# The reciprocal of the softmax sums of an attention kernel, taken in a dense 128x16 layout between DMAs

## What is computed

```
h = layernorm(x) * (1 + ca) + sa                    # x: 4 x 2048 x 512
q, k, v = rope(h @ W_qkv + b_qkv)                   # 16 heads of 32
att = softmax(where(causal, q k^T / sqrt(32), -1e9))
y = (att @ v) @ W_proj + b_proj
x = x + ga * y
```

## Time and profile before

| what | us |
|---|---|
| runs, median of 3 | 3621.95 |
| the profiled execution: span, first to last instruction | 3618.4 |
| its own time | not given apart; the lowest run is 3618.25 |
| PE busy | 3195.3 (88%) |
| DVE busy | 2923.3 (81%) |
| ACT busy | 1780.1 (49%) |
| POOL busy | 1710.6 (47%) |
| DMA, mean share of 16 engines | about 11% |

### The profile page before, as it was taken

One profiled execution on the slowest core, in us unless ns is written; L12 is line 12 of the kernel. 1 busy time (PEld: TensorE's weight loads), 2 busy tenths in 40 slices (PEclk: granted clock), 3 DMA queues, 4 the chain that ended last, 5 costly groups with the idle time before them and its releaser, 6 DMA issues.

```text
span 3618.4 us, 69458 instructions
## 1 busy us (share of the span) xinstructions
PE 3195.3 (88%) x22176; PEld 1266.8 (35%) x22176; DVE 2923.3 (81%) x5670; ACT 1780.1 (49%) x3667; POOL 1710.6 (47%) x1385
## 2 busy tenths in 40 slices
PE   3699999999989989888988989989888999999895
PEld 1324343424343332434334243333424334243221
DVE  4797777897778888898878878888888888888676
ACT  3306565555645454564535545465444545544451
POOL 2403435373526455373653626455363554626454
PEclk8759999999999999999999999999999999999897
DMA  6000000110011000110111001010011010001022
GB/s 213 12 12 4 18 8 7 35 36 15 10 41 40 24 25 27 30 42 21 40 33 41 31 18 42 27 31 25 27 42 47 30 36 21 27 19 36 19 91 73
DMA packets 112229, 124.62 MB, mean 34 GB/s; under 512 B 18276, under 2 KB 85092, under 8 KB 110708
## 3 DMA queue, kind: packets, MB, share of 16 engines
q1 hardware_dynamic: 111864, 120.07, 10.5%
HBM read 83.02 MB, written 36.50 MB: 33 GB/s over the span
## 4 chain that ended last, share of the span: by engine, by line
PE 40%; DVE 31%; issue 13%; DVEq 6%; ACT 2%; POOLq 2%; POOL 2%; DMA 0%; ACTq 0%; SPq 0%
PE ring L1083 10%; DVE mpart L844 9%; PE ps_out L1133 9%; PE ps_scores L1119 7%; PE ps_den L1150 4%; DVE qk L821 4%; PE ps_den L1156 3%; PE ring L1105 3%; DVE wk L888 3%; DVE qk L807 2%; DVE ropeB L829 2%; DVE qk L816 2%; PE ps_scores L1060 2%; DVE dsum L860 2%; DVEq L838 1%
## 5 line engine op out<-in xcount | busy, mean ns | idle before, releaser
L675 ACT ACTIVATE prob<-ps_scores 128x512 f32<-128x512 f32 (+3 forms) x2560 | 1265.7, 537 | 1105.7 <-PE ps_scores L1122 535.0
L844 DVE TENSOR_REDUCE mpart<-ring 128x1 f32<-128x512 f32 (+3 forms) x2560 | 1403.0, 599 | 335.0 <-PE ring L1086 181.7
L483 POOL TENSOR_TENSOR psum<-prob 128x1024 f32<-128x1024 f32 x360 | 866.8, 2429 | 325.5 <-ACT prob L675 163.0
L1083 PE MATMUL ring<-qk 96*128 96x512 f16 (+3 forms) x2560 | 892.3, 368 | 118.1 <-DVE mpart L844 106.3
L1119 PE MATMUL ps_scores<-qk 98*128 98x512 f16 (+3 forms) x2560 | 879.2, 357 | 57.5 <-ACT prob L675 53.6
L1133 PE MATMUL ps_out<-prob,v 128*32 128x512 f32 (+3 forms) x5120 | 609.4, 548 | 6.6 <-ACT qk L635 6.6
L1083 PEld LDWEIGHTS ring<-qk 96*128 96x128 f16 x2560 | 239.7, 99 | 943.8 <-DVE mpart L844 704.4
L1060 PE MATMUL ps_scores<-wg,hT 128*128 128x384 f16 x3072 | 538.3, 328 | 22.9 <-ACT osum L702 9.9
L465 POOL TENSOR_TENSOR ropeA<-qk,cos_sb 128x256 f32<-128x256 f32 x256 | 200.5, 783 | 750.1 <-DVE v L810 745.2
L1119 PEld LDWEIGHTS ps_scores<-qk 98*128 98x128 f16 x2560 | 248.4, 99 | 364.0 <-ACT prob L675 232.9
L1060 PEld LDWEIGHTS ps_scores<-wg,hT 128*128 128x128 f16 x3072 | 292.2, 98 | 200.7 <-issue 18.9
(11 more groups left out here) (127 smaller groups left out, 3134.9 us busy)
## 6 DMA issues: line engine op xcount, KB each, us to landing
xs<-in_L_attn_x_dram SPq DMA_DIRECT2D x124, 256.0 KB, 2.8
attn_out_T<-ot SPq DMA_DIRECT2D x63, 256.0 KB, 2.2
otin<-attn_out_T SPq DMA_DIRECT2D x30, 512.0 KB, 4.6
out_dram<-x SPq DMA_DIRECT2D x60, 256.0 KB, 2.1
wg<-w_qkv_halves SPq DMA_DIRECT2D x16, 768.0 KB, 5.2
qk<-in_L_wmod_dram SPq DMA_DIRECT2D x1, 6144.0 KB, 27.1
bc<-modulation SPq DMA_DIRECT2D x4, 1536.0 KB, 9.1
hT<-in_L_attn_W_qkv_dram SPq DMA_DIRECT2D x1, 3072.0 KB, 10.4
```

The lines of the kernel that those rows point to most:

```text
L483: pool.tensor_tensor(psum2[:, p], prob[:, s % 3, p], prob[:, (s + 1) % 3, p], ALU.add).then_inc(pair_sum, 1)
L675: act.activation(prob[:, s % 3, p, h % 2, 0:w], ps_scores[(HG * s + h) % NBK][:, 0:w], ACT.Exp, scale=SCALE).then_inc(exp_done, 1)
L844: dve.tensor_reduce(mpart[:, h, qt, kc:kc + 1], ring[n % NBK][:, 0:w], AX.X, ALU.max).then_inc(ring_free, 1)
L1083: mm = pe.matmul(ring[n % NBK][:, 0:w], qk[0:R, par, 0, h, qt * P:(qt + 1) * P], qk[0:R, par, 1, h, kc * QC:kc * QC + w], start=True, stop ...
```

## The change

The reciprocal no longer runs over the 128x512 sums with their 32 equal rows a head. Four DMAs take one row of each head and lay it over 32 partitions of a tile `dense`, 128x16 in all (`spread_sums`). DVE takes one reciprocal there (`out_reciprocal`). A DMA writes the result to DRAM as 4 rows of 512, SP waits for that DMA, and another DMA reads each row back into 32 partitions of the sums' tile (`spread_inverses`). POOL's product waits for this. The very last chunk keeps the four reciprocals of before (L1004).

The tables of steps change with it. In LATE `low` goes from 4 to 5 and `store` from 5 to 6, so from steps 3 and 4 of the next group to its steps 4 and 5. `spread` of chunk 3 stands behind all of SP's steps of its group.

`vector_load` counts 0.3 for a step with a reciprocal, where it counted 2.4 for each part, so that the planner places the 160 units otherwise. In a group with five tiles the units of some steps are:

| step | 3 | 6 | 10 | 14 | 20 | 22 | 24 | 26 | 28 | 32 | 38 |
|---|---|---|---|---|---|---|---|---|---|---|---|
| before | 5 | 0 | 1 | 2 | 3 | 5 | 5 | 2 | 1 | 1 | 3 |
| now | 4 | 2 | 0 | 4 | 2 | 4 | 3 | 4 | 4 | 0 | 2 |

The diff, cut to its core:

```diff
-    FAST = {"leave": 0, 0: 1, 1: 1, 2: 2, 3: 2, "norm": 2, "high": 3, "low": 4, "store": 5}
-    LATE = {0: 2, 1: 2, 2: 3, 3: 3, "norm": 3, "high": 4, "low": 4, "store": 5}
-    SLOW = {"leave": 0, 0: 1, 1: 2, 2: 3, 3: 4, "norm": 4, "high": 5, "low": 6, "store": 7}
+    FAST = {"leave": 0, "spread": 0, "recip": 1, "rows": 1, "norm": 2, "high": 3, "low": 4, "store": 5}
+    LATE = {"recip": 2, "rows": 2, "norm": 3, "high": 4, "low": 5, "store": 6}
+    SLOW = {"leave": 0, "spread": 1, "recip": 2, "rows": 2, "norm": 4, "high": 5, "low": 6, "store": 7}
...
-        load = 2.4 * sum(leaving(s, part, False) is not None for part in range(TPC))
+        load = 0.3 * (leaving(s, "recip", False) is not None)
...
+    rows_d = nc.dram_tensor("sum_inverses", (HG, QC), F32, kind="Internal").ap()
...
+        dense = sb("dense", [P, QC // HS], F32)
...
                     for s in range(NS):
+                        cq = leaving(s, "spread", bool(own))
+                        if cq is not None:
+                            spread_sums(NG * b + g, cq)
+                        cq = leaving(s, "rows", bool(own))
+                        if cq is not None and not (cq == NC_ - 1 and g == 0 and first):
+                            spread_inverses(NG * b + g - (cq == NC_ - 1), cq)
                         cq = leaving(s, "store", bool(own))
...
+                    if not (last and g == NG - 1):
+                        spread_sums(NG * b + g, NC_ - 1)
+
+            def spread_sums(G, cq):
+
+                sp.wait_ge(sums_left, NC_ * G + cq + 1)
+                with nc.allow_non_contiguous_dma(reason="one of 32 equal rows a head, 64 B a partition"):
+                    for h in range(HG):
+                        sp.dma_start(dense[h * HS:(h + 1) * HS, :],
+                                     dsum[h * HS:h * HS + 1, :].rearrange("o (j i) -> o j i", j=HS)).then_inc(dense_ld, 16)
+
+            def spread_inverses(G, cq):
+
+                sp.wait_ge(recip_done, NC_ * G + cq + 1)
+                sp.dma_start(rows_d.rearrange("h (j i) -> (h j) i", j=HS), dense[:]).then_inc(rows_st, 16)
+                sp.wait_ge(rows_st, 16 * (NC_ * G + cq + 1))
+                sp.dma_start(dsum[:], rows_d.rearrange("h (o q) -> h o q", o=1).to_broadcast([HG, HS, QC])).then_inc(
+                    rows_ld, 16)
...
             def out_norm(G, cq):
-                pool.wait_ge(recip_done, TPC * (NC_ * G + cq + 1))
+                pool.wait_ge(rows_ld, 16 * (NC_ * G + cq + 1))
...
-            def out_reciprocal(G, cq, part):
-
-                dve.wait_ge(sums_left, NC_ * G + cq + 1)
-                cols = slice(part * P, (part + 1) * P)
-                dve.reciprocal(dsum[:, cols], dsum[:, cols]).then_inc(recip_done, 1)
...
+            def out_reciprocal(G, cq):
+
+                dve.wait_ge(dense_ld, 16 * HG * (NC_ * G + cq + 1))
+                dve.reciprocal(dense[:], dense[:]).then_inc(recip_done, 1)
...
-                        out_parts(G, g, s, (0, 2), first, bool(own))
+                        cq = leaving(s, "recip", bool(own))
+                        if cq is not None and not (cq == NC_ - 1 and g == 0 and first):
+                            out_reciprocal(G - (cq == NC_ - 1), cq)
...
-                        out_parts(G, g, s, (1, 3), first, bool(own))
```

More of the change, by code:

```diff
@@ L251, in adaln_block_kernel @@
             sem(n) for n in ("scores_done", "exp_done", "prob_used", "pair_sum", "pair_used"))
+        dense_ld, rows_st, rows_ld = (sem(n) for n in ("dense_ld", "rows_st", "rows_ld"))
         sums_left, recip_done, out_normed, out_hi, out_split, end_split = (
@@ L854, in maxima @@
                                          ALU.subtract).then_inc(max_split, 1)
-            def out_reciprocal(G, cq, part):
-                dve.wait_ge(sums_left, NC_ * G + cq + 1)
-                cols = slice(part * P, (part + 1) * P)
-                dve.reciprocal(dsum[:, cols], dsum[:, cols]).then_inc(recip_done, 1)
-            def out_parts(G, g, s, parts, first, own):
-                for part in parts:
-                    cq = leaving(s, part, own)
-                    if cq is not None and not (cq == NC_ - 1 and g == 0 and first):
-                        out_reciprocal(G - (cq == NC_ - 1), cq, part)
+            def out_reciprocal(G, cq):
+                dve.wait_ge(dense_ld, 16 * HG * (NC_ * G + cq + 1))
+                dve.reciprocal(dense[:], dense[:]).then_inc(recip_done, 1)
             def tail_product(b, t, use, n):
```

## The result

The changed kernel takes 3646.52 us (median of 4 runs, 3643.30 to 3650.49), the kernel before, on the same chip, 3620.10 us (4 runs). The ratio is 1.0069, with a 95% interval of 1.0057 to 1.0081: **0.7% slower, about 25 us**. The forecast said 3602 us and faster. The range, 3540 to 3660, holds the time, but the direction was wrong. (Of all executions in this text one, of run e3 further down, took 6877.56 us; the figures of that run are without it.)

A forecast was written before the change was run, and what follows sets the result against it. PE was taken to set the pace in plain groups and to wait for DVE's maxima in those with tiles or head work. -86 + 31 + 8 + 14 + 13 = -20 gave 3602 us, range 3540 to 3660.

The forecast's parts named there:

- relief of DVE: Fewer reciprocals on DVE shorten PE's waits for maxima by 81 us, plus 5 us of clock: gain 86 us.
- late `low`: `low` behind POOL's other work in step 4 stalls ACT, then PE, in twelve groups: 31 + 8 us, plus 14 of clock.
- queue of SyncE: In-order waits for reciprocal and store delay loads of attention outputs for tiles: 10 + 3 us.
- head group: Group that prepares the next batch, three of them; DVE busier than PE; 9 of 10.8 us of wait taken as gained.
- the ring's waits: PE waiting for DVE's maxima in the three-bank ring: 10.4 us in a five-tile group, 10.8 head, 12.8 six-tile.
- ceiling of 133 us: Most that freeing DVE can give back: PE's waits for maxima over six five-tile, three head and three six-tile groups, 3.7%.
- load at step 8 of second groups: Attention outputs for a tile, in each batch's second group, land late behind the reciprocal: 3.5 us in three groups, 10 us.
- tile at step 16 of first groups: Its load has the same place in SyncE's queue, with about 1 us missing: 3 us in all.
- hidden part: Sums' way out and inverses' way back fit beside other work; DVE may stand 6 us in all, left to the bounds.
- Rival D: Slow small pieces: each 64-byte crossing takes 4.2 us in place of 2.1, giving 3633 us; chance 0.06.
- C: Slower by the late `low`: stall, clock and pushed pair sums cost 78 us, queue 20 to 30; 3665 us; chance 0.22.
- Plain groups: Three groups without tiles or head work, where PE sets the pace and DVE has room: unchanged at 138 us.

The follow-up runs named there:

- e3: Changed kernel with the planner's old load for reciprocals, so the old distribution of units: 3649.29 us, ratio 1.0070 to the kernel before.
- e4: Kernel before, with each reciprocal over 4 of its 128 columns, no DMA added and no step moved: 3570.97 us, ratio 0.9856.
- e1: Changed kernel with `low` and the store put back one step earlier, where they had been: 3606.51 us, ratio 0.9961 to the kernel before.
- e2: Kernel before with only `low` and the store moved one step later: 3667.53 us, ratio 1.0121.
- e6: Changed kernel with `low` and the store one step earlier and SyncE's tile loads ahead of the way back of the inverses: 3589.14 us, ratio 0.9897.
- e5: Changed kernel with SyncE's tile loads issued ahead of the way back of the inverses, `low` still late: 3638.80 us, ratio 1.0042.
- e7: e6 with the planner's old load for reciprocals, so the old distribution of units: 3573.76 us, ratio 0.9864 to the kernel before.
- e9: e4 with the changed kernel's distribution of units, no DMA added: 3566.86 us, ratio 0.9845 to the kernel before.
- e10: Kernel before, with the second instruction of a tile's second stage on 16 of its 512 columns: 3578.38 us, ratio 0.9879.
- e11: Kernel before, with POOL adding each pair of 128x1024 in two instructions of 128x512: 3567.08 us, ratio 0.9844.

## Why the prediction was wrong

The measured parts, each from a pair of runs, beside the forecast:

| part | forecast, us | measured, us | from |
|---|---|---|---|
| relief of DVE | -86 | -52 | e4 against before |
| late `low`, clock included | +53 | +39 (44 when done alone) | after against e1; e2 against before |
| queue of SyncE | +13 | +23 (10 beside the late `low`) | e1 against e6; after against e5 |
| new distribution of units | 0 | +12 beside the DMAs | e6 against e7 |
| small DMAs themselves | 0 | +3 (19 with the new distribution) | e7 against e4; e6 against e9 |
| sum | -20 | +25 | the whole: +25 |

The first figures form a chain of runs from the kernel before to the changed one (before, e4, e7, e6, e1, after), so it proves nothing that they add up to the whole. What counts is each link, that the late `low` has nearly the same price from both ends, and that other orders give other shares, as the brackets show: the last two rows belong together.

**The step that failed is the gain**, as the prediction put it: "I take half of the wait in a five-tile group", "a little more than half in a six-tile group", "and 9 of the 10.8 us in a head group". It was mis-sized: 86 us against 52. This alone turns the sign: 52 in the sum, with the costs as forecast, gives +14. That the reciprocals take part in the ring's waits was right. But the ceiling of 133 us came from a count of PE's waits, and I took the share that goes as a choice in each kind of group. In e4 the kinds with tiles or head work give 17.0, 10.1 and 15.9 us for 33, 21 and 27. The head group, where I was surest, gains 5 to 6 us, not 9: e7's three take 465.0 us in all against 480.7. DVE being the busier engine there does not make each us of it a us of the group. And in the tile groups the remaining waits stand behind more than I saw: behind second stages that are held by POOL (e10, e11). The 2.07 us that the prediction quotes for L888 are a mean of instructions of 0.75 and of 2.7 us. The lower bound, 44, was nearer to the truth than the value taken.

**The queue** was placed rightly for the load at step 8 of second groups, and sized too low, 13 us against 23 (in the changed kernel itself 10). The tile at step 16 of first groups, for which 3 of the 13 us stand, waits in e3 and not in the changed kernel. The wait of 3.5 us was a slip, the prediction's own terms give 3.2 (2187.5 + 4.6 against 2188.9); measured are 2.1 to 2.6 us, and 3.6 to 5.0 in e1. No clock was charged for these waits. And "landing, at 4.6 us" was taken from a row without a broadcast ahead; the load behind 256 KB took 6.2.

**The planner** was priced at nothing beyond a smaller gain. It costs 12 us beside the DMAs, nothing without them (e9), and nothing is left of it beside the late `low` and the queue (e3). Why is open.

**The late `low`** was right in place, chain, count (12 times) and nearly in size: 2.8 to 3.4 us of ACT's wait for 3.5, 39 to 44 us for 53. The hidden part was right where no load waits and the old distribution stands (e7). Rival D fell, since the pieces take 1.7 and 1.4 us and not 4.2.

Of the rivals **C** decided: slower by the late `low`, on the condition that "the gain would have to be on the low side too". It gave 3665, with a gain of 60 and costs of 103; the costs were 77. I gave it 0.22. By my own bounds a gain between 44 and 66 already meant a loss against costs of 66, and my choice of 86, near the middle, had no row behind it.

Plain groups were to be unchanged and got shorter by 2.6 us each (414.0 to 406.2 for three), in e6 (406.1) and e9 (405.5) too, but hardly in e4 (411.7) and e7 (411.5): the new distribution suits them. I had not looked for that.

## What to carry to other kernels

A change that takes work off a busy engine gives back only the waits that this work ends. Measure that relief alone first (the same instructions on a few columns, as in e4): one run gives about what a design that removes the work can bring with the rest as it is. Then look at what the new steps stand in front of. Here three side effects, one product step moved behind other work on an in-order engine, one queue entry ahead of a load, and a replanned order, turned a gain of 1.4% into a loss of 0.7%, and they are undone by moving a few lines and by giving the planner its old figures back (e7).

## What the runs showed of the hardware

- An instruction of DVE with two SBUF inputs (L888) is held while POOL runs an instruction that reads SBUF, to that instruction's end: of 48, 15 take 750 to 753 ns and 33 take 2340 to 2699 (median of all 2690); with 1/32 of the columns 233 to 237 and 1826 to 2184. How long DVE is held goes by the length of POOL's instruction: with 1024 columns split into two times 512 the median fell to 1600, and the kernel's time by 1.6% though POOL worked 76 us more. I had costed this instruction by its mean and taken it for DVE's own work. DVE's maxima, which read PSUM, kept their mean of 680 ns in both runs, and the reciprocals, with one SBUF input, their median of 942 to 943.
- A reciprocal of 128x128 takes 937 ns, of 128x16 246, of 128x4 164: from the first two, some 6.2 ns a column and 0.15 us a start.
- DMAs of 64-byte pieces landed 1.7 us (2 KB, SBUF to SBUF) and 1.4 us (8 KB, to HBM) after issue. The Trainium skill (DMA: Bandwidth & Descriptors, Specifications) has pieces under 512 B written by read-modify-write. No time that could be put down to it shows here: the pieces land quickly, and e7 is as fast as e4. The 19 us between e9 and e6 have no known cause.
- A load of 512 KB that went out behind a broadcast of 256 KB took 6.2 us to land (median of 30) in place of 4.6, in groups with a DMA share of 11 to 14%; with the loads ahead of the broadcast it was 4.7 again (e5, e6).
